# Second attention in steps of five parts: queries in the first half of a step, the output projection in the second half of the step that turned the heads

## The reference, cut to what matters

```python
x = x + xattn0(layernorm(x), ctx)            # one head of 512
x = x + int8_matmul(layernorm(x), rhs)       # quantised rows, quantised columns
x = x + xattn1(layernorm(x), ctx)            # 16 heads of 32, w_q, w_k, w_v, w_o
x = x + moe(layernorm(x))                    # 8 experts by a sparse mixer, and one shared expert

def xattn1(query, kv):
    q = heads(query @ w_q.T); k = heads(kv @ w_k.T); v = heads(kv @ w_v.T)
    attn = softmax(einsum('bqhd,bkhd->bhqk', q, k) * 32 ** -0.5)
    return einsum('bhqk,bkhd->bqhd', attn, v).reshape(8, 512, 512) @ w_o.T
```

## Time and profile before

| | |
|---|---|
| median of 3 runs | 1240.04 us (1239.22 to 1244.32) |
| the profiled execution's own time | 1242.84 us |
| its span, first to last instruction | 1241.1 us |
| TensorE busy | 1176.2 us (95%) |
| VectorE busy | 932.9 us (75%) |
| ScalarE busy | 662.7 us (53%) |
| GpSimd busy | 539.2 us (43%) |
| chain that ended last | TensorE 84%, VectorE 8%, issue 3%, ScalarE 2% |

### The profile page before, as it was taken

How to read it: one execution, slowest core, us unless ns; L and a number is a source line. 1 busy time by engine, 2 the same in 40 slices (tenths; PEclk the granted TensorE clock), 3 DMA queues, 4 the chain that set the end, 5 groups by cost and what they waited for, 6 DMA issues and landing times.

```text
span 1241.1 us, 28626 instructions
## 1 busy us (share of the span) xinstructions
PE 1176.2 (95%) x10724; PEld 803.1 (65%) x10724; DVE 932.9 (75%) x2080; ACT 662.7 (53%) x1199; POOL 539.2 (43%) x682
## 2 busy tenths in 40 slices
PE   6888998679999999998999999999999999999996
PEld 3555655468888888785444444777777777666663
DVE  5889898879999999886677777767777785745450
ACT  3377778658888888765444322222222231465552
POOL 0037668644555555432100000454555455176745
PEclk9999999989999999999999999999999999999998
DMA  9612014114555555643880050203122514599987
GB/s 346 218 38 100 1 25 55 44 57 143 172 173 170 177 173 178 179 143 104 177 188 6 1 170 18 86 19 86 36 69 44 162 36 109 161 264 232 262 136 96
DMA packets 159033, 150.49 MB, mean 121 GB/s; under 512 B 80017, under 2 KB 112945, under 8 KB 158897
## 3 DMA queue, kind: packets, MB, share of 16 engines
q1 hardware_dynamic: 139904, 122.01, 33.9%
q0 software_dynamic: 14400, 25.35, 9.8%
q10 hardware_dynamic: 4592, 1.32, 0.5%
HBM read 84.93 MB, written 57.19 MB: 115 GB/s over the span
## 4 chain that ended last, share of the span: by engine, by line
PE 84%; DVE 8%; issue 3%; ACT 2%; POOL 1%; DMA 1%; ACTq 0%; SPq 0%; DVEq 0%; POOLq 0%
PE bank L124 30%; PE bank L2232 15%; PE bank L2225 13%; PE bank L1597 6%; PE bank L980 3%; PE bank L1551 3%; PE bank L1528 2%; PE bank L1501 2%; PE bank L1049 1%; PE bank L897 1%; PE bank L1546 1%; PE bank L1544 1%; PE bank L1545 1%; PE bank L916 1%; DVE front_amax L793 1%
## 5 line engine op out<-in xcount | busy, mean ns | idle before, releaser
L1730 POOL DMA_INDIRECT lists<-att_land x128 | 136.9, 1070 | 287.4 <-DVE att_land L1871 169.6
L2225 PE MATMUL bank<-att_land 128*128 128x512 f16 x768 | 176.2, 379 | 0.0
L124 PE MATMUL bank<-program_xs,program_wgu 128*128 128x512 f16 x576 | 130.2, 382 | 0.8 <-DVE att_land L1830 0.8
L2053 ACT ACTIVATE att_land<-program_x 128x512 f32<-128x512 f32 x40 | 25.3, 631 | 195.1 <-DVE program_x L2195 195.1
L2225 PEld LDWEIGHTS bank<-att_land 128*128 128x128 f16 x768 | 75.1, 98 | 81.7
L1216 POOL TENSOR_TENSOR att_land<-att_land 120x512 f16<-120x512 f32 x64 | 74.1, 1158 | 97.9 <-ACT att_land L1401 97.9
L124 PE MATMUL bank<-att_land 128*128 128x128 f16 (+1 forms) x1560 | 107.9, 224 | 3.0 <-DVE att_land L1322 3.0
L124 PEld LDWEIGHTS bank<-program_xs,program_wgu 128*128 128x128 f16 x576 | 56.4, 98 | 68.4 <-issue 1.7
L1597 PE MATMUL bank<-att_land 128*128 128x512 f16 x384 | 98.7, 381 | 1.7 <-DVE att_land L1343 1.7
L1259 DVE TENSOR_REDUCE bank<-bank 128x4 f32<-128x480 f32 x128 | 84.5, 660 | 16.0 <-PE bank L1501 16.0
L124 PEld LDWEIGHTS bank<-att_land 128*128 128x128 f16 x1560 | 91.1, 99 | 5.8 <-DVE att_land L1322 3.4
(11 more groups left out here) (322 smaller groups left out, 2971.9 us busy)
## 6 DMA issues: line engine op xcount, KB each, us to landing
xn_rows<-att_land SPq DMA_DIRECT2D x37, 256.0 KB, 2.7
out_rows<-att_land SPq DMA_DIRECT2D x37, 256.0 KB, 2.6
att_land<-q_rows SPq DMA_DIRECT2D x66, 128.0 KB, 2.6
q_rows<-att_land SPq DMA_DIRECT2D x32, 256.0 KB, 2.0
x_rows<-program_x SPq DMA_DIRECT2D x32, 256.0 KB, 3.0
xt_tiles<-att_land SPq DMA_DIRECT2D x32, 256.0 KB, 2.1
att_land<-x_rows SPq DMA_DIRECT2D x8, 1024.0 KB, 5.5
program_xs<-xt_tiles SPq DMA_DIRECT2D x28, 256.0 KB, 4.9
```

What stands on the lines that cost most here:

```text
L124: last = pe.matmul(out, lhs(a, k), rhs(b, k), start=n == 0, stop=n == len(terms) - 1)
L1730: pool.indirect_dma_start(out=io["lists"], out_offset=bass.IndirectOffsetOnAxis(ap=index[:, t, k:k + 1], axis=0), in_=load[:, t, k, :], in ...
L2225: last = pe.matmul(ps_y[i][:, :], hid[:, c % 2, a, i * P:(i + 1) * P], wd[:, q, c, :], start=c == 0 and n == 0, stop=c == NC - 1 and n == 2)
```

## The change

Steps of second attention have five parts, and run from -7 to 35 instead of from -6 to 36. Against the scores of tile t in step t:
- TensorE: `queries(t + 2)` stand in parts 0 to 2 (first half), `rows_transposed(t + 3)` a step earlier than before, in part 3. `product(t - 2)` stands in part 4, in the step whose part 2 turned the same heads. `gate_transposed` and `gate_logits` come a step earlier (t - 3, t - 4).
- VectorE: `residual(t - 3)`, `gate_stats(t - 3)`, `weighted(t - 2)` and `aggregate(lg, t - 3)` stand in parts 0 and 1; `output_low(t - 2)` stands ahead of `maximum(t, 3)`; `rows_low` and `query_low` stand in parts 3 and 4, ahead of `last_low(t - 1, 3)`.
- GpSimd: `lg.inverse_root(t - 3)` stands between `ln.inverse_root` and `prob_low`, in the step in which VectorE made its statistics.
- ScalarE: `gate_rows(t - 3)`, `query_high(t + 2)` and `output_high(t - 2)` follow each other in part 2. All tiles' rows are normalised by ScalarE (`rows`); `first_rows` is gone.
- SP issues in another order and fetches the shared expert's first rows, one transfer in each of four steps, instead of ScalarE.
- `JOIN` has keys for five parts, on every engine from (-6, 0) on, with the old ticks; its long lines are left out below. `TAIL` is counted in fifths.

```diff
@@ -1108,10 +1088,10 @@
 
 
 def attention1(g, io, m, sem, banks, f):
-    LEAD, LAG = 6, 5
+    LEAD, LAG = 7, 4
+    FETCH = NT - 8
...
     of = g.late(4 * D, [P, D])
@@ -1177,30 +1157,33 @@
                         sp.wait_ge(f.a["exp"], NT)
                         sp.wait_ge(f.q["y_ok"], NT)
                     packed_keys(sp, g, io, b + 1)
-            u = t + 1
+            u, v = t + 2, t - 3
+            if live(v):
+                sp.wait_ge(s["x_new"], v + 1)
+                sp.dma_start(io["x_rows"][v * P:(v + 1) * P, :], g.x[:, v, :]).then_inc(g.x_out.handle, 16)
+                sp.wait_ge(lg.ok, v + 1)
+                sp.dma_start(io["xn_rows"][v * P:(v + 1) * P, :], lg.xn[:, v % 2]).then_inc(rows_out[v % 2], 16)
+            if live(t):
+                sp.wait_ge(s["n_ok"], t + 1)
+                sp.dma_start(g.queries[t % 3][COPIES * DH:ROWS].rearrange("p r (c n) -> p (r c) n", n=P),
+                             shiftT[0:2 * HEADS, :]).then_inc(n_in, 16)
             if live(u):
                 sp.wait_ge(s["q_hi"], u + 1)
                 sp.wait_ge(s["q_lo"], u + 1)
                 sp.dma_start(io["q_rows"][u], qT[:, :, :, :].rearrange("p q k n -> p q (k n)")).then_inc(q_out[u % 2], 16)
-            v = t - 4
+            if live(v):
+                sp.wait_ge(s["g_lo"], v + 1)
+                sp.dma_start(io["xt_tiles"][v, :, :], gT[:, v % 2].rearrange("p q k n -> p (q k n)")).then_inc(gt_out[v % 2], 16)
             if live(u):
                 sp.wait_ge(q_out[u % 2], 16 * (u // 2 + 1))
                 need(sp, c4["t_mm"], KC * (u - 2))
                 if u == 0:
                     sp.wait_ge(f.a["sim"], NT)
                 packed_queries(sp, g, io, u, q_in)
-            if live(v):
-                sp.wait_ge(lg.ok, v + 1)
-                sp.dma_start(io["xn_rows"][v * P:(v + 1) * P, :], lg.xn[:, v % 2]).then_inc(rows_out[v % 2], 16)
-                sp.wait_ge(s["x_new"], v + 1)
-                sp.dma_start(io["x_rows"][v * P:(v + 1) * P, :], g.x[:, v, :]).then_inc(g.x_out.handle, 16)
-            if live(t):
-                sp.wait_ge(s["n_ok"], t + 1)
-                sp.dma_start(g.queries[t % 3][COPIES * DH:ROWS].rearrange("p r (c n) -> p (r c) n", n=P),
-                             shiftT[0:2 * HEADS, :]).then_inc(n_in, 16)
-            if live(v):
-                sp.wait_ge(s["g_lo"], v + 1)
-                sp.dma_start(io["xt_tiles"][v, :, :], gT[:, v % 2].rearrange("p q k n -> p (q k n)")).then_inc(gt_out[v % 2], 16)
+            if FETCH <= t < FETCH + TB:
+                for n in range(2):
+                    sp.wait_ge(gt_out[n], 16 * TB // 2)
+                tokens(sp, g, io, 0, 0, xs_in, [t - FETCH])
 
         def finish():
...
@@ -1230,14 +1213,17 @@
                 pool.tensor_tensor(g.wgu[:, b, 1, :], raw[:, :], g.wgu[:, b, 0, :], ALU.subtract).then_inc(w_part.handle, 1)
 
         def step(t):
-            if live(t - 4):
-                lg.inverse_root(pool, g, t - 4, t % 4)
-            if live(t + 4):
-                ln.inverse_root(pool, g, t + 4, t % 4)
+            if live(t + 5):
+                if t == -5:
+                    pool.wait_ge(f.j_mm, f.jobs)
+                ln.inverse_root(pool, g, t + 5, (t + 5) % 4)
+            yield
+            if live(t - 3):
+                lg.inverse_root(pool, g, t - 3, (t - 3) % 4)
             yield
             prob_low(t - 1, 0)
-            yield
             prob_low(t - 1, 1)
+            yield
             yield
             weights(t)
...
@@ -1351,27 +1330,27 @@
             if t in (-1, 2):
                 key_ones(0 if t < 0 else 1)
             maximum(t, 0)
-            query_low(t + 1)
-            rows_low(t + 2)
+            residual(t - 3)
             yield
             maximum(t, 1)
+            gate_stats(t - 3)
             weighted(t - 2)
+            aggregate(lg, t - 3)
             yield
             maximum(t, 2)
-            residual(t - 3)
+            logits(t - 4)
+            output_low(t - 2)
+            yield
             maximum(t, 3)
             shifts(t)
-            output_low(t - 2)
-            yield
-            gate_stats(t - 3)
+            gate_low(t - 3)
             last_low(t - 1, 2)
-            logits(t - 5)
-            stats(ln, t + 6)
-            aggregate(lg, t - 3)
-            first_rows(t + 3)
+            rows_low(t + 3)
+            yield
+            query_low(t + 2)
+            stats(ln, t + 7)
             last_low(t - 1, 3)
-            aggregate(ln, t + 6)
...
@@ -1445,9 +1424,9 @@
                 lg.shifted(act, g, u, u % 4)
 
         def rows(u):
-            if live(u) and u >= HEAD:
-                if u == HEAD:
-                    act.wait_ge(ln.ok, HEAD)
+            if live(u):
+                if u == 0:
+                    act.wait_ge(f.j_mm, f.jobs)
                 need(act, s["xt_mm"], u - 1)
                 ln.shifted(act, g, u, u % 4)
...
@@ -1459,26 +1438,22 @@
                 act.activation(gT[:, u % 2, 0], ps_g[:, :, :], ACT.Copy).then_inc(s["g_hi"], 1)
 
         def step(t):
-            query_high(t + 1)
-            rows_high(t + 2)
+            yield
             exps(t - 1, 0)
-            yield
-            gate_rows(t - 4)
             exps(t - 1, 1)
             yield
-            rows(t + 3)
+            gate_rows(t - 3)
+            query_high(t + 2)
             output_high(t - 2)
+            yield
             exps(t - 1, 2)
+            gate_high(t - 3)
+            exps(t - 1, 3)
+            rows_high(t + 3)
             shift_copied(t)
             yield
-            exps(t - 1, 3)
-            gate_high(t - 4)
+            rows(t + 4)
             weights_high(t)
-            if t == NT - 6:
-                for n in range(2):
...
         def product(u, k):
@@ -1590,7 +1565,7 @@
             if k == 0:
                 pe.wait_ge(s["o_lo"], u + 1)
                 need(pe, s["x_new"], u)
-                need(pe, s["g_lo"], u - 1)
+                need(pe, s["g_lo"], u)
                 if u == 0:
                     pe.wait_ge(f.q["y_ok"], NT)
             for n, (a, b) in enumerate(PASSES):
@@ -1602,15 +1577,15 @@
         def gate_transposed(u):
             if live(u):
                 pe.wait_ge(lg.ok, u + 1)
-                need(pe, s["x_new"], min(u + 2, NT))
+                need(pe, s["x_new"], u + 1)
                 need(pe, s["g_lo"], u)
                 transposed(ps_g, lg.xn[:, u % 2]).then_inc(s["g_tr"], 1)
 
         def gate_logits(u):
             if live(u):
...
@@ -1621,32 +1596,33 @@
 
         def step(t):
             scores(t, 0)
-            rows_transposed(t + 2)
-            product(t - 3, 0)
+            queries(t + 2, 0)
             yield
             scores(t, 1)
             scores_transposed(t - 1, 0)
-            product(t - 3, 1)
-            product(t - 3, 2)
+            queries(t + 2, 1)
+            queries(t + 2, 2)
             scores_transposed(t - 1, 1)
             yield
             scores(t, 2)
-            product(t - 3, 3)
+            gate_logits(t - 4)
+            queries(t + 2, 3)
             output_transposed(t - 2)
             scores_transposed(t - 1, 2)
+            yield
             scores(t, 3)
             outputs(t - 1, 0)
-            queries(t + 2, 0)
-            queries(t + 2, 1)
-            shift_transposed(t)
-            yield
+            gate_transposed(t - 3)
             scores_transposed(t - 1, 3)
             outputs(t - 1, 1)
-            gate_logits(t - 5)
-            queries(t + 2, 2)
-            gate_transposed(t - 4)
+            rows_transposed(t + 3)
+            shift_transposed(t)
+            yield
+            product(t - 2, 0)
+            product(t - 2, 1)
+            product(t - 2, 2)
             outputs(t - 1, 2)
-            queries(t + 2, 3)
+            product(t - 2, 3)
             outputs(t - 1, 3)
         return step, None
 
@@ -2591,17 +2567,17 @@
...
 JOIN = {"sync": {(-6, 0): 60, (-6, 1): 67},
...
-TAIL = {"sync": [131],
+TAIL = {"sync": [164],
         "gpsimd": [],
-        "scalar": [135, 137, 142, 143],
-        "vector": [135, 139, 150],
-        "tensor": [127, 130, 134, 139, 143, 147]}
+        "scalar": [169, 171, 177, 179],
+        "vector": [169, 174, 187],
+        "tensor": [159, 162, 167, 174, 179, 184]}
...
-            behind = [(s, part) for s in second.steps for part in range(4)]
+            behind = [(s, part) for s in second.steps for part in range(5)]
...
-                if finish and s == NT + 4 and part == 3:
+                if finish and s == NT + 4 and part == 4:
...
-                while places and places[0] <= 4 * s + part:
+                while places and places[0] <= 5 * s + part:
```

More of the change, by code:

```diff
@@ L151, with __init__ @@
 class Norm:
-    def __init__(self, m, name, xn, sb, shift, first=0):
-        self.xn, self.shift, self.first = xn, shift, first
+    def __init__(self, m, name, xn, sb, shift):
+        self.xn, self.shift = xn, shift
```

(27 more changed lines are left out.)

33 lines of the change are left out of this document (12 added, 21 removed).

## The result

The changed kernel takes 1346.49 us (median of four runs, 1344.33 to 1347.34) against 1241.66 us before (median of four runs): 1.0833 times as long, 95% interval 1.0814 to 1.0853. The forecast was 1330, range 1288 to 1372. The profiled execution took 1345.75 us, its span is 1344.0.

The account below looks back on a forecast made before the run. The prediction took TensorE's own work, 10.06 us a step, to bound the kernel before. Its terms: 1242.84 + 76 (stage) + 16 (way in) - 2 (way out) = 1332.8, about 1330 us for the median; range 1288 to 1372.

Parts of the forecast that it names:

- The step: One second-attention step: waits across the engines close a loop from scores to next scores, 12.87 us in place of 10.06.
- The end of the step: Step's last piece: VectorE's second last-low ends at 12.51, then TensorE's last outputs, 0.06 and 0.30, and the next scores.
- The floor of 11.65: Second loop in a step: GpSimd's `prob_low` behind its root, then TensorE's remaining work; the step can't fall below 11.65 us.
- The way in: Start to tile 3's scores: the front runs alone before second attention, 293.2 in place of 277.27, +16 (+7 to +23).
- The last steps: Steps 30 and 31 of second attention: queries and new rows have run out, products still wait for gate low, 12.1 each.
- The way out: Behind second attention: a tile's way has one step less; bounds nothing and 10 us, taken as 2 us less.
- The clock: Rival: TensorE falls to 1.2 GHz a third of the time, +2.4 a step, 70 in all, 1400 us; 10 in 100.
- TensorE's bound: Rival: engines run ahead so far that the step of second attention stays at 10.06, 1250 us; 10 in 100.
- The token stall: Rival: removing step 27's 3.87 us hold of ScalarE's queue by token transfers is what counts, 1234 us; 4 in 100.

Follow-up runs that it names:

- the front alone: Kernel before with the list of places for attention parts among the front's steps left empty, so attention runs after the front: 1258.47 us (before 1240.8).

## Why the prediction was right, and where it was off

- **The step.** 12.87 was worked out, 12.91 measured, and the stations lie where the sum put them: GpSimd's last root instruction ends 5.2 after the scores (493.3), ScalarE's gate rows start at 5.27, output low at 7.09 (worked out as 7.13). VectorE's idle time is 2.58, released by ScalarE; ScalarE's 0.84, released by GpSimd; `prob_low` stands behind the root. Shown by taking parts out: the gate's way in the step of its statistics costs 1.14 a step, the projection's place 0.73, and the orders around them (11.77 to 11.22) 0.55. Each number is the distance to the loop that takes over, in this order of taking out. These three take the step from 12.91 to 10.49; the mean of the same steps before, the stall included, was (563.73 - 277.27) / 28 = 10.23.
- **The end of the step.** The prediction closed the loop over VectorE's last low. The trace closes it as well over gate low and the projection behind it (497.67 to 501.05), a tie: last low ends at 500.68, and the last outputs, which stand behind both, start at 500.74. The prediction's own branch, rows high on ScalarE and rows low at 10.06 (worked out as 10.04), is untouched by an earlier output low; hence moving that alone gained nothing.
- **The floor of 11.65** through `prob_low` was not reached by any run that has the root ahead of it, so no run shows it. With the gate a step later it doesn't hold: 11.44, 11.22 and 10.32 were measured.
- **The way in.** +16 forecast, +17.3 measured; shown by the front alone, +17.7. The sum inside was off in its parts: the front ended sooner than 242.6 (its last product at 238.69, taken as 239.6), and the first queries took 5.30 and 4.46 us in place of 2.7, at a granted clock of 0.62 in that stretch. Tile 0's scores came 1.7 later than the sum has them (261.14, worked out as 259.4); the next three steps took 33.5, where the sum has 33.8 with 5 for the clock. That the whole came so near is in part two errors against each other.
- **The last steps.** The mis-sized term: 12.1 each for steps 30 and 31. Measured were 12.53 and 14.32, and step 29 took 14.07. The granted clock was 0.88, 0.86 and 0.76 in steps 29 to 31, and in step 31 nine products took 3.88 us in place of the 2.10 of the step shown above; the sum had no term for the clock there. TensorE's timeline:

```profile
665.44 3.88 PE L1572 MATMUL bank<-att_land 128*128 128x512 f16 x9 [0.52 <-DVE att_land L1322]
```

  With 1.5 in the 27 steps ahead of them, step 29 among these, this is the 4.1 by which the stage (375.8) exceeds its sum (371.7).
- **The way out.** The step that failed: "I take 2, near nothing", between nothing and a whole step less. It cost 4.3, outside both. The reason given, that the shared expert's products threaded in must run anyway, held, but they are no cover: in TensorE's order they stand behind the gate's transposes and wait with them. From the shared expert's first product to its first one with the second weights, before and after (columns as above):

```profile
572.82:607.29 34.47, 31.26 (x243) 17.12 (x239) 15.93 (x37) 15.84 (x27) 7.65 (x18) 0.96 0.47 163
670.42:709.40 38.98, 30.11 (x218) 15.77 (x215) 17.41 (x37) 15.86 (x26) 9.40 (x18) 0.91 0.51 155
```

  TensorE is busy 1.15 us less and idle 5.66 more (8.87 in place of 3.21). TensorE's timeline after has the waits and what follows them:

```profile
685.73 0.71 PE L1526 MATMUL bank<-program_ident,att_land 128*128 128x128 f32 x4 [2.29 <-DVE program_logits L1327]
686.23 4.40 PE L124 MATMUL bank<-program_xs,program_wgu 128*128 128x512 f16 x12
...
699.25 0.66 PE L1526 MATMUL bank<-program_ident,att_land 128*128 128x128 f32 x4 [3.74 <-ACT att_land L192]
699.74 4.44 PE L124 MATMUL bank<-program_xs,program_wgu 128*128 128x512 f16 x12
```

  Two parts of the shared expert took 4.4 in place of 2.75, 3.3 us together, where one part took 4.03 before: the lower clock makes up about 2 of the difference. The rest of the lost time is the waits; less work than before in this stretch (25 matmul records fewer) takes some 3 back. These shares are read from the rows; no run tried them.
- **Sum.** 17.3 + 80.3 + 4.3 + 1.0 = 102.9, against 90 forecast: 6.3 of the 13 lie in the way out, 4.1 in the stage.
- **The rivals.** The clock: an ordinary step was granted 1.00 with TensorE busy for 11.18 of 13 us. The rule of the Trainium skill cited with that rival (TensorE: Matmul & The Clock Gate, "A second HAM failure mode") would have meant swings in every step; in second attention the rows show a clock below 0.9 only at the two ends, where TensorE had rested longer or the work was running out. TensorE's bound: no, busy for 318 of 376. The token stall: real and gone (step 27 is 12.80), but worth 4.6.

## What to carry to other kernels

Moving work into an earlier step shortens nothing by itself: ask for each result that is now used in the step that makes it which engines it crosses, and add up that chain from the bound engine back to itself. If the chain is longer than the bound engine's work, it is the new step, and the engines' busy shares won't show it. Taking it apart gains only the distance to the next longest chain, so look for that one too before pricing an edit, and whether the edit lengthens it. An idle stretch ahead of one instruction is a place on the loop, not its price: filling it gained nothing here, while taking a result out of its step did.
A hand-written list of places is part of the order: extended by a first entry without a key, it silently turned off the overlap of two stages, for 17 us, of which the one new list that was tried brought back 7.

## What the runs showed of the hardware that was not expected

TensorE's clock held at 1.00 with gaps of 0.1 to 0.7 us in every step, but the stretch on the way in, with idle times of 0.8 to 4.2 us one after another, was granted 0.62, and there 48 matmuls of the queries took 5.30 us, where the prediction's rows at full speed give 2.7. After 3.74 us of idle time the next twelve products took 4.44 in place of 2.75. So a wait can cost more than its own length. The length of the last wait alone doesn't tell when: behind 1.50 us of idle time twelve products took 2.75 (692.58), and in step 29, whose longest wait was 0.95, nine products took 3.44 in place of 2.10 at a granted clock of 0.88.
